# Setup of a fused mLSTM and MLP kernel: maxima first, part of the weight split on TensorE

## The reference

```python
xn = _layernorm(x)
# attention: q, k, v, o_preact = xn @ W.T; gates i, f = 15 * tanh((xn @ W.T + b) / 15)
# per head a scan over time: C = F*C + I*k*v.T, n = F*n + I*k, h = q.C / max(|q.n|, exp(-m))
# y = (sigmoid(o_preact) * (norm(h) * gamma)) @ Wout.T
# mlp: (silu(xn @ w_gate.T) * (xn @ w_up.T)) @ w_down.T
out = x + attention(xn) + mlp(xn)
```

## Time and profile before

| | us |
|---|---|
| median of 3 runs | 3163.22 (3162.7 to 3164.44) |
| the profiled execution | 3165.01 |
| its span, first to last instruction | 3163.3 |
| TensorE busy | 3067.6 (97%) |
| VectorE busy | 1925.3 (61%) |
| ScalarE busy | 1121.3 (35%) |
| GpSimd busy | 771.3 (24%) |
| DMA | 51.08 MB, mean 16 GB/s |

### The profile page before, as it was taken

The page is one execution under the profiler, slowest core; times in us unless marked ns, Lnnn a source line. Parts: engine busy times, 40 slices in busy tenths (PEclk is TensorE's granted clock), DMA queues, the critical chain, the costliest instruction groups (busy, mean ns, idle before and its releaser), DMA issues.

```text
span 3163.3 us, 61615 instructions
## 1 busy us (share of the span) xinstructions
PE 3067.6 (97%) x22426; PEld 2234.5 (71%) x22426; DVE 1925.3 (61%) x4371; ACT 1121.3 (35%) x2142; POOL 771.3 (24%) x1127
## 2 busy tenths in 40 slices
PE   0899999999999999999999999999999999999999
PEld 0677777777777777777777777777777777777776
DVE  8666556666566565566565566665566665665655
ACT  5433333333333333333333233333333333333332
POOL 5321222222222222222222222212222222222222
PEclk9999999999999999999999999999999999999999
DMA  5000000000000000000000000000000000000000
GB/s 220 8 14 13 7 7 13 13 13 13 7 7 13 13 13 13 7 7 13 13 13 13 0 13 13 13 13 7 7 13 13 13 13 7 7 13 13 13 13 7
DMA packets 20333, 51.08 MB, mean 16 GB/s; under 512 B 1506, under 2 KB 1634, under 8 KB 18274
## 3 DMA queue, kind: packets, MB, share of 16 engines
q1 hardware_dynamic: 20322, 50.95, 4.3%
HBM read 34.16 MB, written 16.78 MB: 16 GB/s over the span
## 4 chain that ended last, share of the span: by engine, by line
PE 79%; DVE 13%; issue 4%; ACT 3%; POOL 0%; DMA 0%; ACTq 0%; SPq 0%; DVEq 0%
PE work L1042 17%; PE work L1041 17%; PE work L1040 17%; PE acc L1042 6%; PE acc L1041 6%; PE acc L1040 6%; DVE arena L866 3%; DVE arena L865 3%; PE o_bank L1128 3%; PE o_bank L1187 2%; PE work L1193 2%; DVE arena L913 2%; DVE arena L916 1%; ACT arena L640 1%; DVE amax L707 1%
## 5 line engine op out<-in xcount | busy, mean ns | idle before, releaser
L1040 PE MATMUL work<-xt,weights 128*128 128x256 f16 x4608 | 1257.3, 273 | 0.0
L1041 PE MATMUL work<-xt,weights 128*128 128x256 f16 x4608 | 1257.2, 273 | 0.0
L1042 PE MATMUL work<-xt,weights 128*128 128x256 f16 x4608 | 1257.2, 273 | 0.0
L540 POOL TENSOR_TENSOR arena<-arena 128x256 f16<-128x256 f32 x512 | 348.5, 681 | 1728.6 <-ACT arena L650 1728.6
L913 DVE SCALAR_TENSOR_TENSOR arena<-arena,work 128x256 f32<-128x256 f32 x512 | 215.1, 420 | 539.4 <-ACT arena L646 536.3
L1040 PEld LDWEIGHTS work<-xt,weights 128*128 128x128 f16 x4608 | 479.1, 104 | 69.7
L1041 PEld LDWEIGHTS work<-xt,weights 128*128 128x128 f16 x4608 | 451.4, 98 | 70.0
L1042 PEld LDWEIGHTS work<-xt,weights 128*128 128x128 f16 x4608 | 451.3, 98 | 52.6
L646 ACT ACTIVATE arena<-work,unscale 128x256 f32<-128x256 f32 x512 | 241.1, 471 | 588.3 <-PE work L1042 587.9
L650 ACT ACTIVATE arena<-arena 128x256 f16<-128x256 f32 x512 | 213.3, 417 | 598.9 <-DVE arena L916 598.9
L1040 PE MATMUL acc<-weights,arena 128*128 128x512 f16 x1024 | 388.1, 379 | 0.0
(11 more groups left out here) (193 smaller groups left out, 4036.9 us busy)
## 6 DMA issues: line engine op xcount, KB each, us to landing
arena<-x_dram SPq DMA_DIRECT2D x33, 512.0 KB, 3.4
out_dram<-arena SPq DMA_DIRECT2D x32, 512.0 KB, 2.8
weights<-w_g_dram SPq DMA_DIRECT2D x4, 1024.0 KB, 13.0
weights<-w_u_dram SPq DMA_DIRECT2D x4, 1024.0 KB, 20.6
arena<-w_d_dram SPq DMA_DIRECT2D x4, 1024.0 KB, 26.3
arena<-w_qk_dram SPq DMA_DIRECT2D x1, 1024.0 KB, 6.2
arena<-w_v_dram SPq DMA_DIRECT2D x1, 1024.0 KB, 8.2
weights<-w_o_dram SPq DMA_DIRECT2D x1, 1024.0 KB, 17.4
```

Source lines behind the costliest of these rows:

```text
L540: g.tensor_tensor(hh[:, j % HB, 1, :], tt[:, j % 2, :], hh[:, j % HB, 0, :], ALU.subtract).then_inc(h_ready, 1)
L1040: t.matmul(dst, w[0], a[0], start=first, stop=False, skip_group_check=True)
L1041: t.matmul(dst, w[0], a[1], start=False, stop=False, skip_group_check=True)
L1042: return t.matmul(dst, w[1], a[0], start=False, stop=last, skip_group_check=True)
```

## The change

1. **Order on VectorE in the setup.** All maxima and scales come first; the low parts of `u 2`, `u 3`, `d 0` to `d 3`, `o` and `out` come at the end (`u 2` between the last row maximum and the last scale).
2. **Who makes the low parts.** GpSimd makes five (`qk`, `v`, `g 0`, `g 2`, `u 0`), all early. TensorE makes three (`g 1`, `g 3`, `u 1`): a float32 matmul of a diagonal matrix that holds the scale with the staged piece, less a float16 matmul of a negative identity with the high part, four banks of 512 columns; ScalarE copies the banks into place.
3. **gamma** is no longer multiplied into the staged `out`. Its maximum is taken for each of the four feature groups and multiplied by gamma, and gamma is part of the scale in the high and low parts, in four chunks of 512.
4. **In the loop** `AFTER[3]` is `["wT", "stack3"]` where it was `["stack3", "wT"]`.

The diff's core:

```diff
-AFTER[3] = ["stack3", "wT"]
+AFTER[3] = ["wT", "stack3"]
...
-POOL_LOW = [("v", 0), ("g", 1), ("g", 3), ("u", 1), ("u", 3), ("d", 1), ("d", 3), ("o", 0)]
+POOL_LOW = [("qk", 0), ("v", 0), ("g", 0), ("g", 2), ("u", 0)]
+PE_LOW = [("g", 1), ("g", 3), ("u", 1)]
...
+        amax_out = sb("amax_out", [P, KC], F32)
+        out_scale = sb("out_scale", [P, KC], F32)
+        minus_one = sb("minus_one", [P, P], F16)
+        scale_diag = {n: sb(f"scale_{n}", [P, P], F32) for n in ("g", "u")}
...
+            pool_low("qk", 0)
             pool_low("v", 0)
+            pool_low("g", 0)
...
-            pool_low("g", 1)
+            pool_low("g", 2)
...
-            pool_low("g", 3)
+            pool_low("u", 0)
...
-            pool_low("u", 1)
-            pool.wait_ge(small_loaded, 32)
-            pool.wait_ge(w_loaded["out", 0], 16)
-            for c in range(KC):
-                w = stage["out", 0][:, c * D:(c + 1) * D]
-                g.tensor_scalar(w, w, gam[:, c:c + 1], None, ALU.mult).then_inc(w_gamma, 1)
-            pool_low("u", 3)
...
-            pool_low("d", 1)
-            pool_low("d", 3)
-            pool_low("o", 0)
...
+                elif n == "out":
+                    for c in range(KC):
+                        part = slice(c * D, (c + 1) * D)
+                        s.activation(high(n, k)[:, part], w[:, part], ACT.Copy,
+                                     scale=out_scale[:, c:c + 1]).then_inc(w_hi, 1)
...
+            def low_from_pe(n, k):
+                act.wait_ge(w_low_full, low_done((n, k)))
+                for c in range(KC):
+                    ins = s.activation(low(n, k)[:, c * D:(c + 1) * D], low_banks[c][:, :], ACT.Copy)
+                ins.then_inc(w_split_act, 1)
...
-                act.wait_ge(w_scaled, r + 1)
+                act.wait_ge(w_scaled, r + 2 if names == ["out"] else r + 1)
                 for n, k in pieces(names):
                     high_part(n, k)
+                    if (n, k) == ("g", 2):
+                        low_from_pe("g", 1)
+                    elif (n, k) == ("u", 0):
+                        low_from_pe("g", 3)
+                    elif (n, k) == ("u", 2):
+                        low_from_pe("u", 1)
...
-                    dve.wait_ge(w_gamma, KC)
-                c = ORDER.index((n, k))
+                    link(d.tensor_reduce(amax_out[:, :], stage[n, k].rearrange("p (k f) -> p k f", k=KC), AX.X,
+                                         ALU.max, apply_absolute_value=True))
+                    link(d.tensor_tensor(amax_out[:, :], amax_out[:, :], gam[:, :], ALU.mult))
+                    link(d.tensor_reduce(amax[:, c:c + 1], amax_out[:, :], AX.X, ALU.max, apply_absolute_value=True))
+                    return
                 link(d.tensor_reduce(amax[:, c:c + 1], stage[n, k], AX.X, ALU.max, apply_absolute_value=True))
...
                 dve.wait_ge(w_hi, ORDER.index((n, k)) + 1)
+                if n == "out":
+                    for c in range(KC):
+                        part = slice(c * D, (c + 1) * D)
+                        dve.wait_ge(w_hi, ORDER.index((n, k)) + 1 + c)
+                        ins = d.scalar_tensor_tensor(out=low(n, k)[:, part], in0=staged(n, k)[:, part],
+                                                     scalar=out_scale[:, c:c + 1], in1=high(n, k)[:, part],
+                                                     op0=ALU.mult, op1=ALU.subtract)
+                    ins.then_inc(w_split, 1)
+                    return
...
+            def scale_on_diagonal(n):
+                d.tensor_scalar(scale_diag[n][:, :], ident[:, :], wscale[:, sc[n]:sc[n] + 1], None,
+                                ALU.mult).then_inc(w_diag, 1)
...
             row_maximum(0)
-            maximum("g", 1)
-            scales(0)
             for c in range(NCH):
                 x_low(0, c, (e_bank, s_bank)[c][:, :], xt_ready)
+            scales(0)
+            maximum("g", 1)
             low_part("gates", 0)
             maximum("g", 2)
-            low_part("qk", 0)
             maximum("g", 3)
             own_maximum(1)
             for name, f in (("gates", back / CAP), ("qk", back), ("v", back)):
                 factor(name, f)
             row_maximum(1)
@@ -799,50 +836,55 @@
             link(d.tensor_scalar(unscale[:, NS + 2:NS + 3], wscale[:, sc["qk"]:sc["qk"] + 1], QKS / WS, None,
                                  ALU.mult))
             scales(1)
+            link(d.tensor_scalar(minus_one[:, :], ident[:, :], -1.0, None, ALU.mult))
+            scale_on_diagonal("g")
+            maximum("u", 0)
+            maximum("u", 1)
+            maximum("u", 2)
+            maximum("u", 3)
+            own_maximum(2)
             link(d.tensor_scalar(unscale[:, NS + 3:NS + 4], pow2[:, sc["qk"]:sc["qk"] + 1], 1.0 / QKS, None,
                                  ALU.mult))
             link(d.tensor_tensor(unscale[:, NS + 3:NS + 4], unscale[:, NS + 3:NS + 4], unscale[:, NS + 3:NS + 4],
                                  ALU.mult))
+            row_maximum(2)
             dve.wait_ge(small_loaded, 32)
             link(d.tensor_scalar(bias[:, :], bias[:, :], 1.0 / CAP, None, ALU.mult))
             factor("g", back / 2)
-            maximum("u", 0)
-            low_part("g", 0)
-            maximum("u", 1)
-            maximum("u", 2)
-            maximum("u", 3)
-            own_maximum(2)
-            low_part("g", 2)
-            row_maximum(2)
+            scales(2)
+            scale_on_diagonal("u")
             maximum("d", 0)
-            scales(2)
-            low_part("u", 0)
             maximum("d", 1)
             maximum("d", 2)
             maximum("d", 3)
             own_maximum(3)
-            low_part("u", 2)
+            link(d.tensor_tensor(unscale[:, NS + 1:NS + 2], pow2[:, sc["g"]:sc["g"] + 1],
+                                 pow2[:, sc["u"]:sc["u"] + 1], ALU.mult))
             row_maximum(3)
             maximum("o", 0)
             own_maximum(4)
             scales(3)
             row_maximum(4)
-            link(d.tensor_tensor(unscale[:, NS + 1:NS + 2], pow2[:, sc["g"]:sc["g"] + 1],
-                                 pow2[:, sc["u"]:sc["u"] + 1], ALU.mult))
             link(d.tensor_tensor(unscale[:, NS + 1:NS + 2], unscale[:, NS + 1:NS + 2],
                                  pow2[:, sc["d"]:sc["d"] + 1], ALU.mult))
-            scales(4)
             link(d.tensor_scalar(unscale[:, NS + 1:NS + 2], unscale[:, NS + 1:NS + 2], 2.0 ** 5 / WS, None,
                                  ALU.mult))
-            factor("o", back / 2)
-            low_part("d", 0)
-            low_part("d", 2)
             maximum("out", 0)
             own_maximum(5)
+            scales(4)
+            factor("o", back / 2)
             row_maximum(5)
+            low_part("u", 2)
             scales(5)
+            d.tensor_scalar(out_scale[:, :], gam[:, :], wscale[:, sc["out"]:sc["out"] + 1], None,
+                            ALU.mult).then_inc(w_scaled, 1)
+            dve.wait_ge(w_scaled, len(GROUPS) + 1)
             d.tensor_scalar(unscale[:, sc["out"]:sc["out"] + 1], pow2[:, sc["out"]:sc["out"] + 1],
                             1.0 / (WS * OS * 2), None, ALU.mult).then_inc(w_unscaled, 1)
+            low_part("u", 3)
+            for n in range(4):
+                low_part("d", n)
+            low_part("o", 0)
             low_part("out", 0)
...
+            def low_by_pe(n, k):
+                i_ = low_done((n, k))
+                pe.wait_ge(w_diag, 1 if n == "g" else 2)
+                pe.wait_ge(w_hi, ORDER.index((n, k)) + 1)
+                if i_ > 1:
+                    pe.wait_ge(w_split_act, i_ - 1)
+                for c in range(KC):
+                    part = slice(c * D, (c + 1) * D)
+                    t.matmul(low_banks[c][:, :], scale_diag[n][:, :], staged(n, k)[:, part], start=True, stop=False)
+                    mm_ = t.matmul(low_banks[c][:, :], minus_one[:, :], high(n, k)[:, part], start=False, stop=True)
+                mm_.then_inc(w_low_full, 1)
...
+                if names == ["g"]:
+                    low_by_pe("g", 1)
+                elif names == ["u"]:
+                    low_by_pe("g", 3)
+                elif names == ["o"]:
+                    low_by_pe("u", 1)
+            pe.wait_ge(w_split_act, len(PE_LOW))
```

More of the change, by code:

```diff
@@ L124, with low_done @@
 NPIECES = len(ORDER)
[L125 to L131, removed]
+def low_done(piece):
+    before = ORDER[:ORDER.index(piece) + 1]
+    for own in (POOL_LOW, PE_LOW):
+        if piece in own:
+            return len([p_ for p_ in before if p_ in own])
+    return len([p_ for p_ in before if p_ not in POOL_LOW and p_ not in PE_LOW])
 START = 1
@@ L300, in mlstm_mlp_kernel @@
         w_max_all = sem("w_max_all")
-        w_gamma = sem("w_gamma")
+        w_diag = sem("w_diag")
+        w_low_full = sem("w_low_full")
+        w_split_act = sem("w_split_act")
         w_scaled = sem("w_scaled")
@@ L367, in wait_split @@
```

(35 more changed lines are left out.)

## The result

The changed kernel takes 3146.85 us (median of 4 runs, 3145.82 to 3147.49), the kernel before 3163.81 beside it: ratio 0.9946, 95% interval 0.9932 to 0.9961, **0.54% faster**. The forecast was 3140. The profiled execution took 3146.68, its span 3144.9.

What follows compares the result with a forecast made beforehand. TensorE was taken to bound the loop, a relay ending on VectorE the setup. Setup 10.0, loop order 11.8 and first block 1.5 us, 23.3 off 3163.2, gave 3140 us; range 3133 to 3152.

Steps and rivals of the forecast that it cites:

- The end of the setup: ScalarE's entry into the loop, forecast at 85.8 us instead of 95.8: 10.0 us saved, bounds 14.4 and 4.4.
- the walk: The prediction's step-by-step timing of the new order from profiled durations, putting ScalarE's loop entry at 85.8 us.
- TensorE's low parts: Setup: each low part made by TensorE was to take 6.3 us, 4.4 at full clock and 8.7 at half.
- The factor of 2.3: Setup: each microsecond on TensorE's low part counts 2.3 times, being passed at `g 1` and `u 1`.
- The order in the loop: `wT` first removes TensorE's wait for line 932: 0.38 us in each of 31 blocks, 11.8 us, bounds 13.0 and 6.
- rival 1: Loop: the wait moves to `ffn5`'s bank or the score matmul's stacks instead of going; 3152 us, chance 0.16.
- the tie at `ffn5`: Loop: `ffn5`'s first matmul moves to 221.14, its bank is released at 221.13; losing by 0.2 us gives bound 6.
- The first block: Shorter wait for line 932 gains 1.1 us, plus 0.4 of a possible 1.65 from the half clock: 1.5 us.
- the forecast case: Whole kernel: the summed forecast of 3140 us, own range 3133 to 3147, chance 0.60.
- rival 2: Setup: TensorE's low parts run at half clock throughout, 8.7 us each, entry at 91.4; 3145 us, chance 0.12.
- rival 3: Setup doesn't shrink because VectorE's saved time turns into waiting for ScalarE and TensorE; 3150 us, chance 0.07.
- rival 4: Loop: `wT` first makes VectorE wait for ScalarE's exponential; slower, 3176 us at 2 us late, chance 0.05 with things unseen.

Runs made afterwards that it cites:

- unheld: Changed kernel with minus_one made early, the diagonals of g and u made by ScalarE, and unscale's square behind the row maximum of o: 3143.52 us, ratio 0.9938 to before.
- swap_only: Kernel before with only the loop's order changed (wT ahead of stack3), old setup kept: 3153.10 us, ratio 0.9966 to before.
- before_rows128: Kernel before with the matmul of line 1152 on 128 rows instead of 40: 3159.97 us, ratio 0.9986 to before.
- warm: unheld plus unused float16 matmuls in TensorE's idle time, so the low parts of g 1 and u 1 start at full clock: 3140.54 us, ratio 0.9925 to before.
- setup_only: Changed kernel with the loop's old order (stack3 ahead of wT), new setup kept: 3155.47 us, ratio 0.9975 to before.

## Why the prediction was right in its direction and too large

**The end of the setup (10.0 forecast, 6.85 in the profile).** The last stretch went as walked: from row maximum on, `u 2`, scale, six low parts at 2.27 us, `out`, entry took 21.75 us (67.21 to 88.96) against 21.6 walked. Its start was 3.0 us late, 67.2 for 64.2. The step that failed is the line "the extra scalars and the diagonals, 0.2 us each, are in the walk". The prediction knew that GpSimd lengthens VectorE's low parts and that "The maxima aren't slowed by GpSimd", which is true; what it left out is that a small instruction can be held as long as a large one. Two of them took 2.85 and 3.02. The second one is the whole of what counts up to the scale of u (2.4 to 2.9 us); the first was covered by TensorE's low part, as unheld showed. (The walk's own terms add up to 85.7, not 85.8, which changes nothing.)

The Trainium skill has this in "SBUF — State Buffer", Who interferes with whom: a VectorE instruction with two SBUF inputs waits for a GpSimd one that reads SBUF, in full and not in part, `tensor_scalar` can enter a two-port mode that does too, and `tensor_reduce` never does. By that rule the second instruction would have been priced at the rest of a subtraction, and the first could have been; the saving would have come out about 2.5 us smaller, an estimate from the 2.4 to 2.9 above. The trace agrees for the 2.85 and 3.02 us and for the maxima at 2.3. `tensor_scalar` on one column passed at 0.14. One case goes against the rule: in the trace of before two instructions with two SBUF inputs of one column (lines 830 and 832, at 69.45 and 69.68) took 0.19 and 0.16 us while GpSimd multiplied the staged `out` by gamma (two instructions listed from 67.41 to 70.51), and swap_only and before_rows128 show the same. Why they passed isn't shown.

**TensorE's low parts (6.3, bounds 4.4 and 8.7).** 6.6 for `g 1` and 7.15 for `u 1`. The rates were right, as warm's 4.4 us show. The clock was the open term: the half clock cost 2.2 and 2.75 us, not 1.9. For 59.7 to 64 us the profile grants 0.50; under `g 1` it shows 1.00 from 34 us on although the first two banks go at half the rate, so there the pitch is the better witness, and the low granted clock that the prediction wanted to see at the start didn't show. `g 1` started 0.3 us sooner than walked and so ended in time; the 0.85 us that `u 1` took above 6.3 is the rest of the miss. The factor of 2.3 was near 2: warm made both low parts shorter, by 1.6 and 2.2 us, and gained 3.9.

**The order in the loop (0.38 a block forecast, 0.29 measured).** The wait rows are gone and no other took their place: rival 1 falls, the tie at `ffn5` was won in all later blocks (waits of 0.5 us stand in the first block only). What was mis-sized is the floor: the walk let line 1152 start one pitch behind the last matmul, and the matmul of 40 rows can't. The floor is 0.08 us above that, and 0.04 more between its pair and the next one (0.44 from line 1215 to line 1223, 0.40 from 1152 to 1160 in before). The bounds of 6 and 13.0 held the 9.1 us.

**The first block (1.5 forecast, 2.41).** TensorE was held by the copies, as worked out (0.5 us in front of line 1238), and then by the bank that `ffn5` takes over from `ffn4` (0.5 us in front of line 1082), which wasn't. So the order alone brought 0.7 us (93.90 in setup_only to 93.17), less than the 1.1 forecast. The clock stayed full, which the forecast gave a quarter of its 1.65 us; but in setup_only, with the old order, it did so too. This part of the 2.41 belongs to the run of before that was profiled, and that the forecast was exceeded here is luck.

**The sum.** 3146.85 lies in the range 3133 to 3152 and at the edge of the forecast case's own 3147. Against the median of before beside it the change brought 17.0 of the 23.3 us: about 3 are missing in the setup, 2.7 in the loop, and the first block's share is within the variation of before's own runs. The forecast was made from an execution of the longer group against a median of both.

That the time lies in the range is in part luck: the range was widened for rivals of which none came true. The waits didn't move on (rival 1), the low parts took 6.1 to 7.15 us and not 8.7 (rival 2), the setup did shrink (rival 3) and nothing waits for the exponential (rival 4). The hold that made most of the miss in the setup was in none of them.

## What to carry to other kernels

Before moving small VectorE instructions, look at what GpSimd does at their new time: in this kernel one with two SBUF inputs, or a `tensor_scalar` of 128 columns, waited for the end of a GpSimd subtraction that was already under way, and moving the first away only handed the wait to the next one of its kind. When a wait is removed, the new floor is what the instruction costs without it; here the matmul of few rows had a price that the wait had hidden, and padding it to 128 rows brought more (0.345 us a block) than the reordering itself (0.29). And work handed to an idle TensorE should be priced with its first part at the half clock (6.0 to 7.15 us for 4.4 here), with everything that is queued behind it counted too.

## What the runs showed of the hardware that was not expected

- A VectorE instruction on a single column (two SBUF inputs) took 3.02 us beside a GpSimd subtraction and ended 0.03 us after it; one of 128 columns took 2.85, ending 0.08 after. GpSimd's subtraction was held the same way by VectorE's low part (5.80 us for 4.06).
- A pair of float32 matmuls of 40 rows between matmuls of 128 rows cost TensorE 0.34 us more than the same pair on 128 rows.
- 18 unused matmuls in idle time made the setup 2.3 us shorter, since the low part behind them then ran at the full clock (4.4 us in place of 6.95).
